# Second cross-attention of a two-layer decoder: reciprocals and maxima one step later, one row load in block 3, one maximum instruction for four heads instead of two

## What is computed

```python
H, HD = 16, D // H
scale = HD ** (-0.5)
Q = (q @ Wq + bq).reshape(Bc, Tq, H, HD).transpose(0, 2, 1, 3)
KV = (kv @ Wkv + bkv).reshape(Bc, Tk, 2, H, HD).transpose(2, 0, 3, 1, 4)
K, V = (KV[0], KV[1])
attn = jnp.einsum('bhqd,bhkd->bhqk', Q, K) * scale
attn = jnp.where(key_padding_mask[:, None, None, :], -jnp.inf, attn)
attn = jax.nn.softmax(attn, axis=-1)
out = jnp.einsum('bhqk,bhkd->bhqd', attn, V)
out = out.transpose(0, 2, 1, 3).reshape(Bc, Tq, Dm)
return out @ Wo + bo
...
r = jax.nn.sigmoid(jnp.einsum('btc,dc->btd', xr, W_r))
k = jnp.einsum('btc,dc->btd', xk, W_k)
k_act = jnp.square(jax.nn.relu(k))
out = r * jnp.einsum('btc,dc->btd', k_act, W_v)
...
x = _layernorm(x + _L1_xattn_ref(x, ctx_1024, mask_BxS2_bk0, L1_xattn_Wq, L1_xattn_bq, L1_xattn_Wkv, L1_xattn_bkv, L1_xattn_Wo, L1_xattn_bo), axis=-1)
x = _layernorm(x + _L1_ffn_ref(x, L1_ffn_W_r, L1_ffn_W_k, L1_ffn_W_v, L1_ffn_mu_r, L1_ffn_mu_k), axis=-1)
```

## Time and profile before

| | |
|---|---|
| median of 3 runs | 2286.59 us (2280.58 to 2287.08) |
| the profiled execution's own time | 2283.57 us |
| its span | 2281.8 us, so 1.8 us lie outside it |
| mean granted TensorE clock | 0.956 of full |
| PE busy | 1998.4 us, 88% |
| DVE busy | 1442.5 us, 63% |
| ACT busy | 1205.3 us, 53% |
| POOL busy | 740.0 us, 32% |
| block 4 | from about 1830 to 2281.8 us |

### The profile page before, as it was taken

One profiled execution on the slowest core, in us unless ns is written; L12 is line 12 of the kernel. 1 busy time (PEld: TensorE's weight loads), 2 busy tenths in 40 slices (PEclk: granted clock), 3 DMA queues, 4 the chain that ended last, 5 costly groups with the idle time before them and its releaser, 6 DMA issues. The chain is left out here.

```text
span 2281.8 us, 32747 instructions
## 1 busy us (share of the span) xinstructions
PE 1998.4 (88%) x11278; PEld 1117.6 (49%) x11278; DVE 1442.5 (63%) x2692; ACT 1205.3 (53%) x2757; POOL 740.0 (32%) x1050
## 2 busy tenths in 40 slices
PE   6799999999998899999999886989899967798886
PEld 3344444344443455665555554556576633344444
DVE  4765575576682665657878975667663354567645
ACT  2355655655555465666877861758522324354352
POOL 4360320220010400113553542676551322343323
PEclk8899999999999999999999998999999978899898
DMA  6536444545421100101111123100001356644421
GB/s 154 124 65 147 91 84 91 93 81 88 66 61 43 58 4 5 31 26 39 45 43 45 45 109 118 44 8 29 10 31 53 69 128 118 120 98 97 81 63 39
DMA packets 134047, 156.25 MB, mean 68 GB/s; under 512 B 38090, under 2 KB 104526, under 8 KB 133787
## 3 DMA queue, kind: packets, MB, share of 16 engines
q1 hardware_dynamic: 133882, 154.16, 29.2%
HBM read 98.88 MB, written 46.83 MB: 64 GB/s over the span
## 5 line engine op out<-in xcount | busy, mean ns | idle before, releaser
L952 DVE TENSOR_REDUCE negm_sb<-psA 128x1 f32<-128x640 f32 (+6 forms) x352 | 351.2, 1026 | 180.7 <-PE psA L551 174.1
L729 ACT ACTIVATE pbuf_sb<-psB 128x512 f32<-128x512 f32 (+1 forms) x608 | 329.8, 573 | 229.2 <-PE psB L563 200.5
L1389 ACT ACTIVATE pw_sb<-psA,nmx_sb 128x154 f32<-128x154 f32 x512 | 192.3, 390 | 137.4 <-DVE nmx_sb L1535 137.4
L560 PE MATMUL psB<-qst_sb,kst_sb 99*128 99x512 bf16 (+3 forms) x768 | 234.6, 334 | 19.0 <-issue 6.4
L549 PE MATMUL psA<-kst_sb,qst_sb 96*128 96x512 bf16 (+3 forms) x768 | 195.7, 331 | 7.6 <-DVE negm_sb L952 6.3
L1535 DVE TENSOR_REDUCE nmx_sb<-psA 128x4 f32<-128x616 f32 x128 | 101.9, 796 | 128.3 <-PE psA L1168 128.0
L577 PE MATMUL psO<-pbuf_sb,V_sb 128*32 128x512 f32 (+3 forms) x1536 | 163.7, 506 | 4.4 <-ACT OT_sb L715 2.2
L560 PEld LDWEIGHTS psB<-qst_sb,kst_sb 99*128 99x128 bf16 x768 | 75.1, 98 | 180.6 <-ACT pbuf_sb L729 127.6
L3054 DVE TENSOR_REDUCE negm_sb<-psA 128x2 f32<-128x320 f32 x256 | 115.8, 480 | 67.3 <-PE psA L2817 66.0
L2937 ACT ACTIVATE pb_sb<-psB 128x512 f32<-128x512 f32 x160 | 93.4, 601 | 120.4 <-PE psB L2827 115.2
L2817 PE MATMUL psA<-kst_sb,qst_sb 97*128 97x160 bf16 x512 | 84.1, 253 | 48.5 <-DVE negm_sb L3054 42.6
(11 more groups left out here) (336 smaller groups left out, 4250.1 us busy)
## 6 DMA issues: line engine op xcount, KB each, us to landing
qst_sb<-parts_dram SPq DMA_DIRECT2D x192, 128.0 KB, 4.7
parts_dram<-parts_sb SPq DMA_DIRECT2D x32, 384.0 KB, 2.7
kst_sb<-parts_dram SPq DMA_DIRECT2D x96, 128.0 KB, 7.5
OTC_sb<-OT_sb SPq DMA_DIRECT2D x128, 64.0 KB, 5.8
y_dram<-yw_sb SPq DMA_DIRECT2D x16, 512.0 KB, 2.8
rden_sb<-dens_dram SPq DMA_DIRECT2D x124, 64.0 KB, 2.2
parts_dram<-partsb_sb SPq DMA_DIRECT2D x16, 384.0 KB, 2.7
xT_sb<-xT SPq DMA_DIRECT2D x4, 1024.0 KB, 5.2
```

The source lines that it names most:

```text
L560: last = nc.tensor.matmul(psB[:, k, at:at + hi - lo], kst[0:MAX_ROWS, gg % 3, h, i * P:(i + 1) * P], qst[0:MAX_ROWS, gg % 3, h, lo:hi], st ...
L729: nc.scalar.activation(pbuf[:, key % 2, heads[0]:heads[-1] + 1, lo:hi], psB[:, (nb.n - 1) % 2, 0:len(heads) * (hi - lo)] .rearrange("p (h ...
L952: nc.vector.tensor_reduce(out=negm[:, gg % 2, heads[0]:heads[-1] + 1, j], in_=psA[:, (na.n - 1) % 2, :].rearrange("p (h n) -> p h n", h=le ...
L1389: last = nc.scalar.activation(pw[:, m % 2, h, :], psA[:, m % 2, at:at + K], ACT.Exp, bias=nmx[:, m % 2, h:h + 1], accum_out=psx[:, m % 3, ...
```

## The change

It has four parts.

1. **Reciprocals.** SP's `reciprocals` is cut in two: `denominators` (up to the load into `dens`) stays in unit `gi + 3`, and `inverses` (from the wait for DVE's reciprocal on) goes to unit `gi + 4`; for the last group of a batch both stay in unit `gi + 3`, which is u = 2. DVE's `reciprocals` moves from step 5 of unit `gi + 3` to step 1 of unit `gi + 4`, except for the last group of a batch. POOL's scaling of a batch's first pair moves from step 7 of u = 0 to step 5 of u = 1.
2. **Maxima.** PE's transpose of a group's maxima moves from the end of unit `gg` to the end of step 0 of unit `gg + 1`, DVE's split to step 1 of it, and SP's `move_maxima` from the end of iteration `gg` to iteration `gg + 1`, behind its row and stack loads and ahead of `inverses` and `denominators`.
3. **Rows.** `x1_load_xp(sp, 1)` moves from the start of block 4 to the last stack load of block 3.
4. **One instruction for four heads.** `maxima` waits for both halves (`nf.up(2)`), reads both banks, and frees both at its end (`then_inc(f_free, 2)`). The waits of `first_scores` are unchanged.

```diff
         for j in range(NT):
             for key in side_tasks(gg, j):
                 number_z(key)
-        if gg < GROUPS:
-            number_z(("mx", gg))
+            if j == 0 and 1 <= gg <= GROUPS:
+                number_z(("mx", gg - 1))
...
                 if s == AHEAD + 8:
                     x1_load_stack(sp, 0)
+                    sp.wait_ge(out_stored3[1], 16 * NT)
+                    x1_load_xp(sp, 1)
...
-            def reciprocals(gi):
+            def denominators(gi):
...
                 sp.dma_start(dens[:, :], dens_dram[0].rearrange("h (a n) -> (h a) n", a=P // 4)).then_inc(dens_loaded, 16)
+
+            def inverses(gi):
+
                 sp.wait_ge(inv_made, gi + 1)
...
-            x1_load_xp(sp, 1)
...
                     load_xe(q - 1)
+                if 1 <= gg <= GROUPS:
+                    move_maxima(gg - 1)
+                if 0 <= gg - 4 < GROUPS and gg % G != 3:
+                    inverses(gg - 4)
                 if 0 <= gg - 3 < GROUPS:
-                    reciprocals(gg - 3)
+                    denominators(gg - 3)
+                    if gg % G == 2:
+                        inverses(gg - 3)
...
-                if gg < GROUPS:
-                    move_maxima(gg)
...
             def transpose_maxima(gg):
-                pe.wait_ge(f_free, nf.n)
+                pe.wait_ge(f_free, 2 * NT * (gg + 1))
...
-                if gg < GROUPS:
-                    transpose_maxima(gg)
+                    if j == 0 and 1 <= gg <= GROUPS:
+                        transpose_maxima(gg - 1)
...
-                    if j == 7 and 0 <= gg - 3 < GROUPS and (gg - 3) % 2 == 1:
+                    if j == 7 and 0 <= gg - 3 < GROUPS and gg % G == 2:
                         scale_values((gg - 3) // 2)
+                    if j == 5 and 0 <= gg - 4 < GROUPS and gg % G == 1:
+                        scale_values((gg - 4) // 2)
...
-            def maxima(gg, j, half):
-                if j == 0 and half == 0 and gg >= 2:
+            def maxima(gg, j):
+                if j == 0 and gg >= 2:
                     dve.wait_ge(zc_full, ZC_SLOT[("mx", gg - 2)])
-                dve.wait_ge(f_full, nf.up())
-                nc.vector.tensor_reduce(out=negm1[:, gg % 2, 2 * half:2 * half + 2, j],
-                                        in_=psA[:, 0, half * 512:half * 512 + 2 * KP].rearrange("p (a n) -> p a n", a=2),
-                                        axis=AX_X, op=ALU.max, negate=True).then_inc(f_free, 1)
+                dve.wait_ge(f_full, nf.up(2))
+                nc.vector.tensor_reduce(out=negm1[:, gg % 2, :, j].rearrange("p (h a) -> p h a", h=2),
+                                        in_=psA[:, 0, :].rearrange("p (h x) -> p h x", h=2)[:, :, 0:2 * KP].rearrange(
+                                            "p h (a n) -> p h a n", a=2),
+                                        axis=AX_X, op=ALU.max, negate=True).then_inc(f_free, 2)
...
-                    if gg < GROUPS:
-                        maxima(gg, j, 0)
+                    if j == 1 and 1 <= gg <= GROUPS:
+                        split_max(gg - 1)
...
                     if gg < GROUPS:
-                        maxima(gg, j, 1)
+                        maxima(gg, j)
...
-                    if j == 5 and 0 <= gg - 3 < GROUPS:
+                    if j == 5 and 0 <= gg - 3 < GROUPS and gg % G == 2:
                         reciprocals(gg - 3)
+                    if j == 1 and 0 <= gg - 4 < GROUPS and gg % G != 3:
+                        reciprocals(gg - 4)
...
-                if gg < GROUPS:
-                    split_max(gg)
```

## The result

The changed kernel takes 2292.86 us (median of 20 runs, 2285.07 to 2300.80), the kernel before 2281.24 us in the runs beside them (20 runs, 2275.11 to 2290.59). The ratio is 1.0048, 95% interval [1.0036, 1.0060]: 11 us slower. The forecast was 3 us faster, with 0.23 for slower. The time lies in the range of 2262 to 2297 us, but on the other side of no change. Four slow executions, of 2486 to 3829 us, are left out of all medians and ratios.

What follows compares the result with a forecast made beforehand. PE was held up in block 4 by DVE, which stood still for denominators from DRAM. Terms -4.8 - 15.1 - 3.4 + 5 - 5 + 20 = -3.3 gave 2280 us from 2283.57, 8-in-10 range 2262 to 2297.

Steps and rivals of the forecast that it cites:

- rows `XP`: Start of block 4: PE's 4.81 us wait for these rows goes and nothing similar stands behind it; -4.8 us.
- reciprocals: DVE asks later in groups 0, 1, 2, 4: stalls -15.1, clock -3.4, last groups of batches served later +5 us.
- maxima moved: Unit boundaries: PE needs the same maxima anyway, with some gain where the split was slow; -5 us, bounds 0 and -10.
- merged maximum: One buffer makes PE and DVE take turns in bare steps; +20 us, bounds 0 and +36.
- bare step: A step without a filler of 1 us or more: 1.60 us against 0.92, so 0.68 more.
- the bare steps of the prediction's list: 26 steps in units 0 to 6 and 12 to 14, counted as 24 x 0.68 = 16.3 us.
- 0.4 us a step for `rv`: The whole maximum stands behind the normalisation before PE goes on: two steps in each of 4 units, 3.2 us.
- +5 for all later groups: Last group of each batch served later: +2 us in unit 6, +1 each in units 10, 14 and 18.
- so I add nothing: Unit 3: maxima behind the XP load on SP reach PE about when PE gets there; no added time.
- The bound of +20: Upper bound for serving the last groups of batches later: 4 x 5 us where nothing covers it.
- SP's queue: Rival: in units 3, 6, 7, 10, 14 maxima and inverses wait behind 8 us loads; +10, 2290 us, chance 0.12.
- The single buffer in the filled steps: Rival: units 7 to 15, 0.4 us in each of 32 more `o` or `rv` steps; +13, 2293 us, chance 0.18.

Runs made afterwards that it cites:

- the split move: The change with two maxima, SP storing the maxima, then serving inverses, then loading the maxima, XE left in place: 2269.37 us, 0.9955 of the kernel before.

## Why the prediction was wrong

| term | forecast | alone, by its run |
|---|---|---|
| rows `XP` | -4.8 | -5.5 |
| reciprocals | -13.5 | +3.6 |
| maxima moved | -5 | +3.4 |
| merged maximum | +20 | +21.0 |
| all four | -3.3 | +11.0 (the change itself) |

The right column is the ratio less 1, times 2281. The single parts add up to +22.6, the change has +11.0, since the reciprocals and the maxima's move help each other: with the rows they come to -6.4 (two maxima kept), where their single runs add up to +1.6.

1. **The rows** were right in mechanism and size.
2. **The merged maximum** was right in mechanism, and its total is partly luck. The loop of a bare step was put at 1.60 us and measured 1.65 in the step shown, +0.73 where +0.68 stood: DVE starts 0.11 us behind PE's last score where 0.04 stood, and PE 0.06 behind DVE where 0.08 stood (0.10 by the times beside it). In the changed kernel the merge cost 17.4 us (1.0048 less 0.9972) against 20. From the trace with two maxima to that of the changed kernel, the bare steps of the prediction's list, without step 6 of unit 6, are 17.4 us longer, where 16.3 stood. Not in the working were the clock and the place of the maximum. The clock falls in units 2 to 5 without any long idle time, which the prediction named as unpriced; the steps with `values` in units 3 and 5 are 6.7 us longer, and the run with second scores first bought unit 3's share back. The maximum behind the normalisation was priced at 0.4 us a step for `rv` and nothing for `o`; moved ahead of it, it gave 6 us. What offset them are stalls that a later PE no longer sees: step 6 of unit 6 is 5.8 us shorter than with two maxima, step 2 of units 1 and 2 together 4.4. The Trainium skill (VectorE: DVE Perf Modes, "Rules for kernel authors") asks for few DVE operations. On DVE this trace agrees: its busy time fell by 9.8 us (1442.5 to 1432.7). The kernel got slower by the merge all the same, because PE waited for the buffer, of which the rule says nothing.
3. **The step that failed is the one on the reciprocals and the maxima's move**, -18.5 together against a measured -0.9 (two maxima kept, less the rows). The failed sentences are "So group 3's reciprocal comes about 2 us later than 1953.30", with +5 for all later groups, and, for the maxima, "so I add nothing" on SP. The stalls named as gone went: by the reciprocals alone units 3, 5 and 7 gained 12.4 us, where 18.5 stood with the clock. But the reciprocals alone cost 13.9 us in units 6, 10, 11, 14 and 15, where +5 stood, and 2.7 us in unit 4 for transfers that had been hidden by the stall. The price of one small return trip was taken from its median of 1.4 us, whereas in this place it stands behind 1 MB or six stack loads and takes 5.4 to 8.6 us. That row was on the page of the prediction itself: the store issued at 1943.12 behind `XE` let the chain go on only at 1950.83. The maxima's return was then put ahead of the same chain, another 5.5 to 8 us. The bound of +20 held the 13.9; the value inside the bound was wrong. A second cost of the maxima's move was not seen either: the split behind the normalisation, 3 us in step 1 of unit 10.
4. **The rivals.** SP's queue, at 2290 with 0.12, was the nearest to what happened, with units 6, 10 and 14 named among its places; its 10 us is most of the 14 us between the forecast (3 us faster) and the result (11 us slower). The single buffer in the filled steps, at 2293 with 0.18, has nearly the time, but not by its mechanism: it wanted 0.4 us in each of 32 more steps, and from the trace with two maxima to the changed one steps 2 to 7 of the three units with `o` are longer by 2.8 us in all, some by 0.65 and others shorter.

Shown by runs: the size of each part, the merge's two side costs, that a small transfer is late beside the 1 MB on either queue, and that SP's row binds unit 6 (17.8 us of chain cut to 11.0, step 6 from 14.8 to 3.9 us, 0.9972 to 0.9911). Only argued: how much of that is SP's waiting in series and how much the transfers ahead of it, and how the -0.9 us of both parts divides among all their places. The split gave 4, 8 and 9 us in its three pairs; `XE` away from its place gave 5 us without the split and 9 to 10 with it. The intervals within most of these pairs touch.

The best version beats both kernels: the change with two maxima, the split move, and `XE` on ScalarE's queue, 0.9911 [0.9884, 0.9938] of the kernel before, 1.4% under the changed one. The one with `XE` a unit earlier on SP's queue is as good within the intervals.

## What to carry to other kernels

Before two operations are merged, look at what each of them frees: two halves that came free one by one let two engines overlap, and one instruction for both makes them take turns. A stall that goes sends the engine to the next late thing sooner, so follow it through the following units, and price every return trip at its new place, by a row with the same transfers under way, on its own queue or another, not by its median. To get a large load out of its way, ask for it early enough that it has landed. Where a queue's engine waits for a store before it issues the next thing, store first, serve others, and wait last.

## What the runs showed of the hardware

- A 24 KB store came back to SP after 5.4 to 5.7 us behind six loads of 128 KB, and after 7.4 to 8.6 us where 1 MB had been asked for as well; two small stores behind the same 1 MB came back within 0.2 us of each other. A 16 KB store of inverses took 7.3 to 8.0 us behind the 1 MB, 5.7 us behind six stack loads, and 1.4 us by its median before.
- The other engine's queue did not keep a small transfer out of the way. With the 1 MB asked for by ScalarE at 2100.22 us, a 16 KB load that SP asked for 1.0 us later took 5.9 us and landed with it; with the 1 MB landed it took 1.9 us.
- The granted clock fell to 0.50 though PE had not been idle for more than 1.5 us at a time in the 10 us before; from 1876 to 1880 it was busy half of the time. With a shorter turn (1.43 us a bare step, not 1.65) it stayed at 1.00 through the same unit.
